# Eight batches through attention and expert layers: the experts' content as two half sums in column tiles

## The reference, cut to what matters

```python
spikes_enc = jax.nn.sigmoid(layernorm(x) @ enc_W + enc_b)      # 512 x 512
cont = spikes_enc @ s2c_W + s2c_b                              # 512 x 64
logits = jnp.tanh(cont @ rW1 + rb1) @ rW2 + rb2                # 8 experts, the best 2 gated
h = jax.nn.relu(jnp.einsum('nm,emh->enh', cont, We1) + be1)
expert_out = jnp.einsum('enh,ehm->enm', h, We2) + be2
output = jnp.einsum('enm,ne->nm', expert_out, gates)
decoded = jax.nn.sigmoid(jax.nn.sigmoid(output @ c2s_W + c2s_b) @ dec_W + dec_b)
```

## Time and profile before

| | |
|---|---|
| median of 3 runs | 1747.21 us (1744.1 to 1747.36) |
| the profiled execution | 1746.18 us, span 1743.3 us |
| TensorE busy | 1591.9 us, 91% |
| VectorE busy | 1285.2 us, 74% |
| ScalarE busy | 785.6 us, 45% |
| mean granted TensorE clock | 0.980 |

### The profile page before, as it was taken

The page is one execution under the profiler, slowest core; times in us unless marked ns, Lnnn a source line. Parts: engine busy times, 40 slices in busy tenths (PEclk is TensorE's granted clock), DMA queues, the critical chain, the costliest instruction groups (busy, mean ns, idle before and its releaser), DMA issues. The chain is left out here.

```text
span 1743.3 us, 28682 instructions
## 1 busy us (share of the span) xinstructions
PE 1591.9 (91%) x10784; PEld 895.6 (51%) x10800; DVE 1285.2 (74%) x3138; ACT 785.6 (45%) x1473; POOL 137.1 (8%) x155
## 2 busy tenths in 40 slices
PE   4689899999999989999999999999999998998976
PEld 2163564545555365554755456553655546454533
DVE  5969867896679866798668966898667985646723
ACT  1043445535364444644355353644436443563633
POOL 1020110001101020000100011010200001000000
PEclk9899999999999999999999999999999999998989
DMA  9040350014301152021600134001520216004000
GB/s 325 18 158 14 138 167 2 16 73 158 99 2 48 40 186 71 4 87 63 194 2 16 73 138 119 2 29 59 182 74 4 87 51 189 7 11 138 13 3 12
DMA packets 50262, 133.98 MB, mean 77 GB/s; under 512 B 6256, under 2 KB 22576, under 8 KB 45520
## 3 DMA queue, kind: packets, MB, share of 16 engines
q1 hardware_dynamic: 50128, 132.16, 23.0%
HBM read 80.99 MB, written 46.04 MB: 73 GB/s over the span
## 5 line engine op out<-in xcount | busy, mean ns | idle before, releaser
L1308 DVE TENSOR_TENSOR arena_AB<-qT,kT 128x2048 f32<-128x2048 f32 (+3 forms) x240 | 399.4, 1715 | 9.4 <-PE bank L1606 5.0
L1363 DVE CUSTOM_DVE_ANT_0 bank<-bank,causal_b 128x512 f32<-128x512 f32 (+3 forms) x512 | 233.6, 523 | 130.7 <-PE bank L1680 130.2
L1524 PE MATMUL bank<-arena_F,kept 128*128 128x512 f32 (+1 forms) x544 | 255.9, 615 | 13.9 <-DVE arena_F L1453 9.5
L1606 PE MATMUL bank<-arena_AB,slot_w 128*32 128x512 f32 x1408 | 200.0, 614 | 34.0 <-DVE arena_AB L1308 32.1
L1120 ACT ACTIVATE arena_AB<-bank 128x512 f32<-128x512 f32 (+1 forms) x352 | 166.9, 586 | 78.3 <-PE bank L1694 78.3
L1524 PEld LDWEIGHTS bank<-arena_F,kept 128*128 128x128 f32 (+1 forms) x544 | 99.6, 192 | 140.4 <-issue 117.1
L1153 ACT ACTIVATE arena_F<-bank,kept 128x512 f32<-128x512 f32 x256 | 160.4, 705 | 18.1 <-PE bank L1524 16.1
L1800 PE MATMUL bank<-kept,arena_F 128*128 128x256 f32 x512 | 116.2, 381 | 6.6 <-ACT arena_F L1170 6.6
L1785 PE MATMUL bank<-arena_F,kept 128*64 128x512 f32 x512 | 119.4, 600 | 2.2 <-ACT arena_F L1153 1.0
L1524 PE MATMUL bank<-xnT,kept 128*128 128x512 f32 x256 | 115.5, 604 | 4.4 <-ACT xnT L1045 2.7
L988 POOL TENSOR_TENSOR rstd_F<-var_eps_F,minus_half 128x4 f32<-128x4 f32 x32 | 34.3, 1072 | 971.3 <-DVE var_eps_F L1238 971.3
(11 more groups left out here) (191 smaller groups left out, 2420.9 us busy)
## 6 DMA issues: line engine op xcount, KB each, us to landing
arena_AB<-band SPq DMA_DIRECT2D x32, 1344.0 KB, 6.4
arena_AB<-stacks SPq DMA_DIRECT2D x64, 384.0 KB
stacks<-arena_AB SPq DMA_DIRECT2D x48, 256.0 KB, 2.8
band<-arena_AB SPq DMA_DIRECT2D x32, 328.0 KB, 3.6
stacks<-xnT SPq DMA_DIRECT2D x32, 256.0 KB, 2.6
band<-kT SPq DMA_DIRECT2D x4, 1352.0 KB, 22.0
stacks<-xn SPq DMA_DIRECT2D x16, 256.0 KB, 2.4
kept<-kept_pack SPq DMA_DIRECT2D x1, 3797.0 KB, 18.7
```

The lines of the kernel that those rows point to most:

```text
L1308: ins = nc.vector.tensor_tensor(prod[SET_AT[i]][:, col:col + c, :], qT[:, hf, :].unsqueeze(1).broadcast_to([P, c, T]), k, ALU.mult)
L1363: ins = nc.vector.tensor_tensor_reduce(out=s, in0=s, in1=causal[:, (TT - 1 - i) * P:T], scale=-1.0, scalar=BIG, op0=ALU.add, op1=ALU.min, ...
L1524: ins = nc.tensor.matmul(out(ps), w, x, start=n == 0, stop=n == len(pairs) - 1)
L1606: ins = nc.tensor.matmul(ps[HS * col:HS * (col + 1), :], slot_w[:, slot(n), :], prod[SET_AT[i]][:, col, :], start=r == 0, stop=False, skip ...
```

## The change

The product over four blocks becomes two half sums: blocks 0 and 1 into partitions 0 to 63 of one bank, blocks 2 and 3 into partitions 64 to 127, with 64 weight columns each, alternating between the halves of the array (`halves`). ScalarE copies the bank to `moe_t`. A new `cont` multiplies it by `pair_sum`, a matrix made of four identities of 64, which adds the two halves and puts the sum on both. `pair_sum` is made in the setup by two sums of halves of the identity; `ones` moves into the end of the expert arena. The planner's costs follow, `halves` counts as tiled, and the constants of the planner (tick, depth, offsets) are others, so that every queue's order may differ.

```diff
-    p.put("cont", ("PE", 3.43, *[("enc", m, "ACT") for m in range(KF)]), ("ACT", 1.15), ("DVE", 0.6))
+    p.put("halves", ("PE", 1.72, *[("enc", m, "ACT") for m in range(KF)]), ("ACT", 0.6))
+    p.put("cont", ("PE", 0.86, ("halves", "ACT")), ("ACT", 1.15), ("DVE", 0.6))
...
-TICK, DEPTH = 0.078, 0.23
+TICK, DEPTH = 0.028, 0.72
...
-    ("A", "ACT"): {"sT": 730},
-    ("A", "DVE"): {"prod": 2330},
-    ("A", "PE"): {"tS": 1545.8, "pA": -2110, "pr": -630},
-    ("B", "DVE"): {"S": 1140, "pr": 330},
-    ("B", "PE"): {"turn": 1070, "S": 2980, "ST": 590, "pr": 230},
-    ("F", "ACT"): {"hid": 1230},
-    ("F", "DVE"): {"lg": 2160, "eo": -1470},
-    ("F", "PE"): {"turn": 740, "hid": 983.2, "dec": 4990},
+    ("A", "ACT"): {"sT": -110, "pA": 220},
+    ("A", "DVE"): {"prod": 3830},
+    ("A", "PE"): {"prod": -740, "tS": 930, "pA": -1340, "on": -330, "pB": -440, "oNT": -180, "pr": -270},
+    ("B", "PE"): {"qk": 690, "S": 3410, "ST": 550},
+    ("F", "ACT"): {"hid": -1460},
+    ("F", "DVE"): {"cont": -820, "gates": -660},
+    ("F", "PE"): {"turn": 1310, "hid": 240, "dec": 7220},
...
-    "A": [-4050, 2690, 0, 0, -446.1, 0, 0, 0],
-    "B": [0, 0, 0, 0, 0, 0, -630, 0],
-    "F": [0, 0, 0, 0, 0, 0, 109.2, 0, 0, 0, 0, 0, 0, -1500, 0, 0],
+    "A": [-8100, 0, 0, 0, 0, 0, 0, 0],
+    "B": [0, 0, 0, 0, 0, 0, 0, 120],
+    "F": [0, 0, 0, 0, 0, 0, 0, 0, 0, 0, 0, 0, 0, -630, 510, 0],
...
-    return kind in ("prod", "PV", "eo") or u.stage == "A" and kind == "oT"
+    return kind in ("prod", "PV", "eo", "halves") or u.stage == "A" and kind == "oT"
...
-DVE_SETUP = 26
+DVE_SETUP = 28
...
+        pair_sum = sb("pair_sum", [P, P])
...
-        ones = sb("ones", [P, P])
...
+        ones = arena["F"][:, ARENA["F"] - P:ARENA["F"]]
...
+                elif kind == "halves":
+                    act.wait_ge(*bank_full(u, "halves"))
+                    ps, read = place(u, "halves")
+                    nc.scalar.copy(moe_t, ps[:]).then_inc(read, 1)
...
+                    for half in range(2):
+                        once(nc.vector.tensor_tensor(pair_sum[:, half * M:(half + 1) * M], ident[:, 0:M], ident[:, M:P], ALU.add))
...
+                elif kind == "halves":
+                    for x in covered(u, name, [("enc", m) for m in range(KF)]):
+                        pe.wait_ge(*bank_read(u, x))
+                    pe.wait_ge(*bank_free(u, name))
+                    ps, full_ = place(u, name, full)
+                    for k in range(2):
+                        for half in range(2):
+                            ins = nc.tensor.matmul(ps[M * half:M * (half + 1), :], s2c_w[:, 2 * half + k, 0:M],
+                                                   t_enc[:, 2 * half + k, :], start=k == 0, stop=k == 1)
+                    ins.then_inc(full_, 1)
                 elif kind == "cont":
-                    product(u, name, lambda ps: ps[:], [(s2c_w[:, k, :], t_enc[:, k, :]) for k in range(KF)],
-                            read=[("enc", m) for m in range(KF)])
+                    product(u, name, lambda ps: ps[:], [(pair_sum[:], moe_t)], read=["halves"])
```

## The result

The kernel after takes 1773.1 us (median of 4 runs, 1768.8 to 1777.8) against 1747.3 us of the kernel before: a ratio of 1.0143, with an interval of 1.0119 to 1.0167. It is 26 us slower where 9 us faster was forecast, and it lies outside the range.

The account below looks back on a forecast made before the run. TensorE was taken as the bound, nearly without holes in the middle. Product savings passing through, less last call and setup, gave 6.5 us; the new order 2.5; together 9.0 off, hence 1738.2 us, range 1726 to 1750.

Parts of the forecast that it names:

- the order anew: All queues replanned with new tick, depth and offsets: gain taken as 2.5 us, at most 13, loss at most about as much.
- The cost of the product: TensorE at `halves` and `cont`: each call saves 0.63 us beside scores, 0.54 beside slot products; 8.8 us over fifteen calls.
- two full drains: TensorE's tiling switches around `halves`: estimated 0.35 us a call, 3.2 us more over sixteen calls than the rows give.
- The copy and the last call: ScalarE's copy between `halves` and `cont`: 0.60 us, covered elsewhere; last call's chain 3.85 us against 3.71, losing 0.14.
- Passing through: Share of TensorE's saving reaching the time: all 5.0 us beside scores, half beside products, 1.9 of 3.8.
- the third rival: The gain stays a wait: VectorE paces seven calls, switches cost more, the order gives nothing; 1745 us, chance 0.14.
- Setup: Two 128x64 sums on VectorE before `small` ends: 0.25 us for both together, bounds 0 and 1.4.
- The slower one: New order empties the end, bare expert chains: 1757 us with two, 1749 with one; last-stretch idle above 52; chance 0.19.

Follow-up runs that it names:

- e13: Kernel after, expert-call stores issued ahead of the band read, plus a 384-column VectorE reduction between variance and slot product at 13 places: 1750.1 us.
- e7: Kernel after with SP's store of an expert call issued ahead of the band read that preceded it in the queue, nothing else moved: 1755.2 us.
- e14: Kernel before with a 384-column VectorE reduction between variance and slot product, only at the causal calls' statistics, six places: 1742.1 us.
- e8: Kernel after in its own order, half sums replaced by the full four-matmul sum, addition by an identity product, copy kept: 1799.8 us.
- e12: Kernel before's old product with the new tick, depth and offsets, and the expert-call store issued ahead of the band read: 1766.4 us.
- e1: New product with the old constants, planner ties broken by each block's position in the order of the kernel before: 1753.7 us.
- e9: Kernel after, expert-call stores issued ahead of the band read, plus a 128-column VectorE reduction between variance and slot product at 13 places: 1763.1 us.

## Why the prediction was wrong

**The step that failed is "the order anew": a gain of 2.5 us, bounded at 13 either way.** Measured with the old product it is a loss of 29.6 us. The bound was built from TensorE's recurring waits, as if a new order could only remove them or have as many more. It could do what no such row holds:

- It brought a store up against a band read on SP's queue. That costs 17.9 us in the kernel after. The prediction never read the queue of the transfers. What bounds such a cost stands there: a 512 KB store of 3.0 us, a 1344 KB read of 6.4 us, five times, with a load, the statistics, a power and the normalised rows behind them.
- It took away a wait of 0.35 us that stood in before between six second norms of expert calls and the slot products behind them, so that 13 powers are slow instead of 7. With none slow (their means are 1010 and 1011 ns in e13) the time is 5.1 us less. The slow ones stood in the trace of before, 2.98 against 1.01 us, and were not looked at.
- It has other holes. With both remedies the new kernel stands at 1750.1, and before with its spacer at 1742.1. If the product is worth the 10.1 us that TensorE is busy less in e7, and if the two add up, the rest of the order still costs some 18. In the traces TensorE waits 43.1 us for the slot products in e13 and 30.7 in e14, and 11.8 against 3.5 for ScalarE's copies of near weights. VectorE still waits 18 times for the power of an expert norm in e13, 20.3 us, against 8 times and 8.8 us in e14: at eleven more places than in before what is next in its queue needs the power itself. At 430 us, for one, a copy of a bank stands in between in before and nothing in e13. Which position in the order makes these waits, and which of them cost time, was not tried. VectorE's waits in e13:

```profile
DVE arena_F L1494 <- POOL rstd_F L1006: 11.3, 10, 1.1
DVE arena_F L1274 <- POOL rstd_F L1006: 9.0, 8, 1.1
```

**The cost of the product was right.** Forecast were 0.63 and 0.54 us a call, measured are 0.73 and 0.69: the new `cont` takes 0.91 and 1.05, less than the `rh` it was priced by. `halves` takes the 1.87 of the row. By the Trainium skill's page "TensorEngine Tiling (Array Packing)" (section Key Properties) a change of tiling mode drains TensorE; no more of it shows here than that row already held. The prediction's estimate of two full drains comes to 16 x (0.35 - 0.16) = 3.0 us, not 3.2.

**The copy and the last call were right.** The copy takes 0.585 us, forecast 0.60, and TensorE waited for it once, 0.7 us. The last call of after, from the start of `halves` to the reader of `cont`:

```profile
1723.41 1.94 PE L1761 MATMUL bank<-arena_F,kept 128*64 128x512 f32 x8 [0.98 <-ACT arena_F L1138]
1725.38 0.58 ACT L1143 COPY arena_F<-bank 128x512 f32<-128x512 f32 x1 [2.23 <-PE bank L1761]
...
1726.02 1.13 PE L1531 MATMUL bank<-arena_F,pair_sum 128*128 128x512 f32 x2 [0.67 <-ACT arena_F L1143]
1727.18 0.69 ACT L1147 ACTIVATE arena_F<-bank,s2c_bias 128x512 f32<-128x512 f32 x1 [1.22 <-PE bank L1531]
```

That is 3.77 us, forecast 3.85.

**Passing through** was set at half beside the products and all of it beside the scores. That is 6.9 of 8.8 us, four fifths. In the new order it holds: e8 paid 26.7 us for 25.0, or some 20, four fifths, if the clock's part is taken off. e12 against e7 shows 11, with the change of order in it. In an order close to that of before (93% of TensorE's blocks) it is less than nothing: e1 lost 5.5 us, with TensorE busy 1.0 us less and idle 13.6 us more. That a saving turns into waits for VectorE (39.81 and 39.66 of 40 us) is the third rival. In e1 these waits grew by 4.0 us for the slot products and 6.2 among the scores, but the rival's time was 1745 and e1 takes 1753.7, so it doesn't cover the case. Why e1 is slower, and not the same, is not settled.

**Setup**, 0.25 us, can't be told apart in the time of any run; in the trace of after the two sums take 0.224 us each.

**The rivals.** The slower one named the end: idle above 52 us in the last stretch, two bare chains. It is 49.5 (the prediction's 45.7 for before counts 0.7 us behind the end of the span; it is 45.0), and the lost time lies in the middle, so it was the wrong mechanism with the right sign. The sign of a change of order was thought to follow from TensorE's rows; what is shown of it came from two resources whose rows were not read.

## What to carry to other kernels

Where an order is planned anew, one part of the bound is what the planner doesn't know: here the length of a store that meets a long read in its queue, and of a GpSimd instruction that meets a VectorE one. Read the rows of SP, of the DMA queues and of GpSimd for an instruction whose time differs from case to case, and ask how many more of the slow kind a new order could make. And try a change of a block and the order made anew as two kernels: the order alone was worth 30 us, the block with the shifts that it caused gained 5 to 11 in two orders and lost 5 in another, and no pair of runs here has the new block alone in exactly the order of before.

## What the runs showed of the hardware that was not expected

- **A power of 128x4 elements on GpSimd** takes 1.01 us, or 2.98 when it begins 0.17 us behind a VectorE product of 2.28 us with two inputs. Beginning 0.03 us ahead of the product doesn't help it (3.17 us); 0.28 us does. The product is never slower itself. One small instruction of VectorE in between made the kernel before faster: e14.
- **A store of 512 KB** frees its home after 3.0 us alone and 7.7 to 8.2 us when a band read is in flight ahead of it on the same queue; issued 0.56 us ahead of that read it takes 3.7.
- **TensorE's clock** was lower in two stretches of e9 than in the same of e7, with the same order of work but for the spacers. The windows of e9, then the same of e7 (the last three columns are the granted clock, the DMA share, GB/s):

```profile
845.00:875.00 30.00, 29.92 (x334) 23.02 (x327) 16.19 (x53) 11.64 (x22) 7.27 (x10) 0.89 0.65 182
...
1052.00:1100.00 48.00, 44.52 (x397) 29.98 (x397) 26.17 (x93) 16.44 (x30) 7.32 (x10) 0.93 0.46 133
```

```profile
845.00:875.00 30.00, 28.35 (x357) 21.43 (x356) 19.99 (x64) 12.19 (x24) 7.28 (x10) 1.00 0.73 216
```

Up to 843 us e9 was ahead of e7 by 4.1 us (its third store left at 843.57, that of e7 at 847.70); at 1261 it was 5.1 us behind (1261.19 against 1256.10). In between its clock was 0.89 and 0.93 on average in these two stretches, part of the time at 1.2 instead of 2.4 GHz (0.50 from 845 to 850 us); in e7 it was 1.00 in both. Before the first fall TensorE waited 1.57 us for VectorE, to 844.77; at the same place e7 waited 1.57 us too, to 848.91, and its clock stayed at 1.00. The runs of e9 lie between 1754.1 and 1764.6 us, the two fastest at the highest clocks (0.982 and 0.980). So some of its 8 us on e7 probably is such a fall; what brings it on was not tried.
